# Attention with mixture-of-experts on one core: a constant scale in the exponential, a reordered front, and 25 of 71 expert tiles spread over three steps

## The reference

```python
Q = apply_rope(proj(W_q)); K = apply_rope(proj(W_k)); V = proj(W_v)      # 16 heads of 8
attn = softmax(Q @ K.T / sqrt(8)); attention = (attn @ V) @ W_o.T
w, idx = top_k(xn @ Wg, 2); w = softmax(w)                                # 8 experts, 2 a token
h = relu((layernorm(xn) * gamma[e] + beta[e]) @ W1[e] + b1[e])           # 128 -> 512
expert = h @ W2[e] + b2[e] + xn                                          # 512 -> 128
out = x + attention + sum of w * expert over the two experts
```

## Time and profile before

| | us |
|---|---|
| median of 3 runs | 660.07 |
| lowest, highest run | 659.75, 661.24 |
| the profiled execution's own time | 659.6 |
| span of its profile | 657.7 |
| PE busy, ACT busy, DVE busy in it | 608.5, 548.6, 384.1 |

### The profile page before, as it was taken

The page is one execution under the profiler, slowest core; times in us unless marked ns, Lnnn a source line. Parts: engine busy times, 40 slices in busy tenths (PEclk is TensorE's granted clock), DMA queues, the critical chain, the costliest instruction groups (busy, mean ns, idle before and its releaser), DMA issues.

```text
span 657.7 us, 12339 instructions
## 1 busy us (share of the span) xinstructions
PE 608.5 (93%) x4649; PEld 256.8 (39%) x4649; DVE 384.1 (58%) x1117; ACT 548.6 (83%) x552; POOL 226.1 (34%) x261
## 2 busy tenths in 40 slices
PE   8789889988999999999999999999999999888884
PEld 6223312213545454434454545443444545111112
DVE  4854687888555555587655555558765564335112
ACT  2678899998788888888888888888888888999993
POOL 4399900027753433332433343333234221100000
PEclk9989999999999999999999999999999999999997
DMA  6156411002201202000220120200012111530000
GB/s 229 27 164 179 117 32 33 1 9 53 61 18 29 57 29 57 25 21 17 57 62 17 30 57 29 57 25 21 17 53 54 29 21 45 225 137 32 1 1 34
DMA packets 25425, 35.60 MB, mean 54 GB/s; under 512 B 5472, under 2 KB 15760, under 8 KB 24848
## 3 DMA queue, kind: packets, MB, share of 16 engines
q1 hardware_dynamic: 19936, 23.70, 11.9%
q0 software_dynamic: 4608, 9.45, 5.0%
q10 hardware_dynamic: 816, 1.61, 0.7%
HBM read 17.43 MB, written 8.91 MB: 40 GB/s over the span
## 4 chain that ended last, share of the span: by engine, by line
PE 63%; ACT 22%; DVE 8%; issue 2%; SPq 2%; DMA 1%; DVEq 1%; POOL 0%; ACTq 0%
PE acc L613 23%; ACT ring L825 22%; PE bank L665 11%; PE sc L580 11%; PE bank L657 9%; PE bank L650 2%; PE bank L511 2%; SPq L303 2%; PE bank L674 1%; DVE xn L1169 1%; DVE turned L1148 1%; DVE work L1182 1%; DVE rotated L867 1%; DMA wr<-L_attn_W_k 1%; DVE hl L863 1%
## 5 line engine op out<-in xcount | busy, mean ns | idle before, releaser
L825 ACT ACTIVATE ring<-sc,exp_scale 128x1024 f32<-128x1024 f32 x512 | 534.5, 1130 | 83.2 <-PE sc L580 82.3
L613 PE MATMUL acc<-ring,v 128*9 128x512 f32 x2048 | 268.8, 597 | 2.5 <-issue 2.5
L580 PE MATMUL sc<-qs,ks 32*128 32x512 f16 x1024 | 147.2, 386 | 28.6 <-ACT ring L825 27.4
L456 POOL DMA_INDIRECT token_out<-work,token x72 | 78.4, 1089 | 155.4 <-DVE work L1189 149.1
L446 POOL DMA_INDIRECT work<-normed,token x72 | 70.1, 973 | 159.2 <-DVE work L1175 95.0
L580 PEld LDWEIGHTS sc<-qs,ks 32*128 32x128 f16 x1024 | 40.0, 91 | 145.3 <-ACT ring L825 110.7
L665 PEld LDWEIGHTS bank<-xn,work 128*128 128x128 f32 x576 | 69.7, 191 | 65.1 <-DVE work L1182 37.7
L1182 DVE TENSOR_SCALAR work<-bank,xn 128x128 f32<-128x128 f32 x288 | 80.9, 343 | 22.9 <-PE bank L657 22.8
L665 PE MATMUL bank<-xn,work 128*128 128x128 f32 x576 | 83.2, 287 | 3.1 <-DVE work L1175 3.0
L657 PE MATMUL bank<-work,xn 128*128 128x128 f32 x576 | 77.2, 277 | 2.1 <-DVE norms L888 1.3
L1169 DVE COPY xn<-w_all 128x1158 f32 x72 | 56.5, 785 | 33.2 <-DVE work L1189 32.3
(11 more groups left out here) (175 smaller groups left out, 336.5 us busy)
## 6 DMA issues: line engine op xcount, KB each, us to landing
w_all<-L_ffn_W SPq DMA_DIRECT2D x16, 256.0 KB, 4.9
qs<-hl SPq DMA_DIRECT2D x60, 64.0 KB
ks<-hl SPq DMA_DIRECT2D x60, 64.0 KB
x<-L_attn_x SPq DMA_DIRECT2D x4, 512.0 KB, 7.9
normed<-xn SPq DMA_DIRECT2D x4, 512.0 KB, 3.3
xn<-token_out SPq DMA_DIRECT2D x2, 1024.0 KB, 6.8
w_all<-token_out SPq DMA_DIRECT2D x2, 1024.0 KB, 11.6
out<-x SPq DMA_DIRECT2D x8, 256.0 KB, 2.3
```

The source lines that it names most:

```text
L456: pool.indirect_dma_start(out=y_d[:, :], in_=ys[done % TILE_BUFFERS], in_offset=None, out_offset=bass.IndirectOffsetOnAxis(ap=token[:, 1, ...
L580: last = nc.tensor.matmul(dst, ks[r:r + 32, kb * P:(kb + 1) * P], qs[r:r + 32, at], start=True, stop=not slow)
L613: last = nc.tensor.matmul(acc[qh % 2][32 * j:32 * j + VW, :], v9[:, b, kb, 4 * g + j, :], ring[:, (2 * n + j // 2) % UNITS, j % 2, :], sta ...
L825: nc.scalar.activation(ring[:, (2 * n + u) % UNITS, :, :], sc[u][:, :].rearrange("p (h c) -> p h c", h=2), ACT.Exp, scale=exp_scale[:, 0:1 ...
```

## The change: edits and diff

- The exponential's scale is a number, `SCALE / 2**14`, and not the tile `exp_scale`; ACT no longer waits for it. To allow that, `gains` limits the power for k so that both powers multiply to 2**14 (one more chained DVE instruction and one unchained); `missing_gain` (3 instructions) stands in place of `scales` (4) and tells by `no_room` whether they do; the flag of batch 0 is multiplied by it, and `decide` has one instruction less for later batches. Only the slower branch changes otherwise (it works on widened copies of q and k).
- Front: for piece 0 the plain product comes before the rotated one, on PE and DVE, and its square on ACT with it; the rotated product of piece 3 is made behind `head_norms`; `project_plain` is made before step 0's scores, not in step 0. Six fewer warming matmuls. On POOL, the clearing of `shift` is first, the sorting of `wo` is before the three low parts, and the normalising is x*a+b with an offset made by two more small instructions a batch. Moments of batches 2 and 3 move on DVE to steps 3 and 5, `tops` of batch 0 from step 4 to 8.
- Experts: 71 tiles. 25 of them (tiles 18 to 27, 42 to 51 and 66 to 70, where the step within the batch is from 28 to 61, batch 0 excepted) have three steps: `tile_in(t+1)` and three quarters of `layer_one(t)`; its last quarter and half of `layer_two(t-1)`; the other half. The last expert step is 235 in place of 212. Of the plain steps 101 to 113 and 165 to 177 each now stands between two three-step groups. The flags of batches 2 and 3 are one step later (122, 186).
- End: `LOAD_AT` becomes 237, the merges stand at 241, 244, 247 and 250; the first half of the last batch's projection (step 252) waits on DVE for all merges.

```diff
-GAIN_EXPONENT = 127 + 12 + 63
+SCORE_BITS = 14
+TOP_EXPONENT = 127 + 12 + 63
 ROPE_ORDER = ((0, 0), (0, 1), (1, 0), (1, 1))
-WARM = (10, 18)
-SLOT_TILES = 72
+WARM = (10, 12)
...
-TOP_AT = {4: 0, 11: 1, 15: 2, 19: 3}
+MOMENTS_AT = {3: 2, 5: 3}
+TOP_AT = {8: 0, 11: 1, 15: 2, 19: 3}
...
+FFN_FROM = 54
 FREE_STEPS = [n for n in range(FFN_FROM, STEPS) if n not in PLAIN_AT and n not in PROJECT_AT]
+TWO_STEPS = (((0, FC), None), (None, (0, FC)))
+THREE_STEPS = (((0, 3), None), ((3, FC), (0, 2)), (None, (2, FC)))
 FIRST, SECOND, WEIGHTS_AT = {}, {}, {}
 used = 0
 for t in range(SLOT_TILES):
-    FIRST[FREE_STEPS[used]] = t
-    used += t < SLOT_TILES - DENSE_TILES
-    SECOND[FREE_STEPS[used]] = t - 1
-    WEIGHTS_AT[FREE_STEPS[used]] = t + 2
-    used += 1
-SECOND[FREE_STEPS[used]] = SLOT_TILES - 1
-SECOND = {n: t for n, t in SECOND.items() if t >= 0}
-WEIGHTS_AT = {n: t for n, t in WEIGHTS_AT.items() if t < SLOT_TILES}
+    n = FREE_STEPS[used]
+    wide = n > PER_BATCH and n % PER_BATCH in LONG_IN and FREE_STEPS[used + 1] == n + 1
+    for one, two in THREE_STEPS if wide else TWO_STEPS:
+        if one:
+            FIRST[FREE_STEPS[used]] = (t, *one)
+        if two and t > 0:
+            SECOND[FREE_STEPS[used]] = (t - 1, *two)
+        used += 1
+    if t + 2 < SLOT_TILES:
...
-MERGE_AT = {LOAD_AT + 8 + 5 * b: b for b in range(B)}
+MERGE_AT = {LOAD_AT + 4 + 3 * b: b for b in range(B)}
...
             nc.gpsimd.memset(v9[:, :, :, :, DK:VW].rearrange("p b k h o -> p (b k h) o"), 1.0).then_inc(v_one, 1)
+            nc.gpsimd.memset(shift[:, :], 0.0).then_inc(shift_zero, 1)
             nc.gpsimd.memset(small[:, 10, :], -0.5).then_inc(pool_step, 1)
...
+            def offsets(ts):
+                after(nc.gpsimd.tensor_tensor(small[:, 9, ts], mv[:, ts, 0], small[:, 6, ts], ALU.mult))
+                after(nc.gpsimd.tensor_scalar(small[:, 8, ts], small[:, 9, ts], -1.0, None, ALU.mult))
             def normed(t):
-                nc.gpsimd.tensor_scalar(xn[:, t, :], x[:, t, :], mv[:, t, 0:1], small[:, 6, t:t + 1],
-                                        ALU.subtract, ALU.mult).then_inc(xn_pool, 1)
+                nc.gpsimd.tensor_scalar(xn[:, t, :], x[:, t, :], small[:, 6, t:t + 1], small[:, 8, t:t + 1],
+                                        ALU.mult, ALU.add).then_inc(xn_pool, 1)
             for h in range(2):
                 ts = slice(4 * h, 4 * h + 4)
...
+            nc.gpsimd.tensor_copy(wo_by_head[:, :].rearrange("o (j g d) -> o j g d", j=4, g=4),
+                                  wr[:, 3, :].rearrange("o (g j d) -> o j g d", g=4, j=4)).then_inc(wo_sorted, 1)
             for i, r in enumerate((0, 3, 2)):
                 c, s = ROPE_ORDER[r]
...
-            pool.wait_ge(wo_in, 16)
-            nc.gpsimd.tensor_copy(wo_by_head[:, :].rearrange("o (j g d) -> o j g d", j=4, g=4),
-                                  wr[:, 3, :].rearrange("o (g j d) -> o j g d", g=4, j=4)).then_inc(wo_sorted, 1)
-            nc.gpsimd.memset(shift[:, :], 0.0).then_inc(shift_zero, 1)
...
             pe.wait_ge(bank_taken[1], USE["second half",])
-            for r in range(2):
-                project_front(sc[r][:, CH:2 * CH], r, 1).then_inc(proj, 1)
-                project_front(sc[r][:, 0:CH], r, 0).then_inc(proj, 1)
+            project_front(sc[0][:, 0:CH], 0, 0).then_inc(proj, 1)
+            project_front(sc[0][:, CH:2 * CH], 0, 1).then_inc(proj, 1)
+            project_front(sc[1][:, CH:2 * CH], 1, 1).then_inc(proj, 1)
+            project_front(sc[1][:, 0:CH], 1, 0).then_inc(proj, 1)
...
+            pe.wait_ge(rope_rot, 1)
             project_front(sc[0][:, 0:CH], 2, 0).then_inc(proj, 1)
-            project_front(acc[1][:, :], 3, 1).then_inc(proj, 1)
             values(0, 1)
             pe.wait_ge(head_ok, 1)
             head_norms(0)
+            project_front(acc[1][:, :], 3, 1).then_inc(proj, 1)
             values(0, 2)
             check_bound(0)
             values(0, 3)
...
-                pe.wait_ge(w_ok, t + 1)
-                pe.wait_ge(bank_taken[1], USE["tile", t])
-                enter_bank(0, "one", t)
-                for c in range(FC):
+            def layer_one(t, c0, c1):
+                if c0 == 0:
+                    pe.wait_ge(w_ok, t + 1)
+                    pe.wait_ge(bank_taken[1], USE["tile", t])
+                    enter_bank(0, "one", t)
+                for c in range(c0, c1):
                     last = nc.tensor.matmul(bank[0][:, c * P:(c + 1) * P], w_tile[t % 3][:, c * P:(c + 1) * P],
                                             xsT[t % 2], start=True, stop=True)
...
-            def layer_two(t):
-                pe.wait_ge(bank_taken[0], USE["one", t])
-                enter_bank(1, "two", t)
-                for c in range(FC):
+                if c1 == FC:
+                    last.then_inc(bank_full[0], 1)
...
                         project_rotated()
                     if n == 0:
...
-                                         ACT.Exp, scale=exp_scale[:, 0:1]).then_inc(e_ok, 1)
+                                         ACT.Exp, scale=SCALE / (1 << SCORE_BITS)).then_inc(e_ok, 1)
...
-                nc.vector.tensor_scalar(gain[:, :].bitcast(I32), half_exp[:, :], -float(1 << 23),
-                                        float(GAIN_EXPONENT << 23), ALU.mult, ALU.add).then_inc(gain_ok, 1)
...
-            def scales():
-                link(nc.vector.tensor_scalar(ungain[:, :].bitcast(I32), half_exp[:, :], float(1 << 23),
-                                             float((254 - GAIN_EXPONENT) << 23), ALU.mult, ALU.add))
-                link(nc.vector.tensor_tensor(bound_scale[:, 0:1], ungain[:, 0:1], ungain[:, 1:2], ALU.mult))
-                nc.vector.tensor_scalar(exp_scale[:, 0:1], bound_scale[:, 0:1], SCALE, 1e30, ALU.mult, ALU.min
-                                        ).then_inc(scale_ok, 1)
-                nc.vector.tensor_tensor(bound_scale[:, 1:2], bound_scale[:, 0:1], bound_scale[:, 0:1], ALU.mult
-                                        ).then_inc(scale_ok, 1)
+                nc.vector.tensor_scalar(room[:, :], half_exp[:, 0:1], float(127 + SCORE_BITS - 12 - 63), None,
+                                        ALU.add)
+                link(nc.vector.tensor_scalar(gain_exp[:, :], half_exp[:, :], -1.0, float(TOP_EXPONENT), ALU.mult,
+                                             ALU.add))
+                link(nc.vector.tensor_tensor(gain_exp[:, 1:2], gain_exp[:, 1:2], room[:, :], ALU.min))
+                nc.vector.tensor_scalar(gain[:, :].bitcast(I32), gain_exp[:, :], float(1 << 23), None, ALU.mult
+                                        ).then_inc(gain_ok, 1)
+            def missing_gain():
+                link(nc.vector.tensor_tensor(no_room[:, :], room[:, :], gain_exp[:, 1:2], ALU.subtract))
+                nc.vector.tensor_scalar(missing[:, :].bitcast(I32), no_room[:, :], 127.0, float(1 << 23), ALU.add,
+                                        ALU.mult)
...
-                    link(nc.vector.tensor_scalar(flag_f[:, 0:1], flag_f[:, B:B + 1], (SAFE / SCALE) ** 2, None,
-                                                 ALU.is_le))
+                    link(nc.vector.scalar_tensor_tensor(out=flag_f[:, 0:1], in0=flag_f[:, B:B + 1],
+                                                        scalar=(SAFE / SCALE) ** 2, in1=no_room[0:1, :],
+                                                        op0=ALU.is_le, op1=ALU.mult))
...
-                v.wait_ge(proj, rotated_made)
-                times(rotated[:, :], rotated_of, r, sin)
+                if rotated_made < plain_made:
+                    v.wait_ge(proj, rotated_made)
+                    times(rotated[:, :], rotated_of, r, sin)
                 v.wait_ge(proj, plain_made)
                 v.wait_ge(sq_ok, i + 1)
                 times(turned[r % 2][:, :], plain_of, r, cos).then_inc(rope_out, 1)
+                if rotated_made > plain_made:
+                    v.wait_ge(proj, rotated_made)
+                    times(rotated[:, :], rotated_of, r, sin).then_inc(rope_rot, 1)
+                    v.wait_ge(rope_rot, 1 if i == 0 else 2)
                 add_up(i, r)
...
             link(split_high(1))
             nc.vector.tensor_tensor(hl[:, 1, 1, 0:CH], turned[1][:, :], hl[:, 1, 0, 0:CH], ALU.subtract
                                     ).then_inc(low_dve, 1)
...
+            missing_gain()
             bound(0)
             decide(0)
...
+                nc.vector.tensor_scalar(wide[0][:, :], qs[:, :], missing[:, :], None, ALU.mult).then_inc(m_wide[b], 1)
+                nc.vector.tensor_copy(wide[1][:, :], ks[:, :]).then_inc(m_wide[b], 1)
                 for n in range(4 * TB):
                     v.wait_ge(m_mm[b], 4 * TB * base + n + 1)
...
+                if b == B - 1:
+                    v.wait_ge(merged, B)
...
+                if n in MOMENTS_AT:
+                    moments_of(MOMENTS_AT[n])
...
-                    if FIRST[n] + 1 < SLOT_TILES:
```

(32 more changed lines are left out.)

71 lines of the change are left out of this document (44 added, 27 removed).

## The result

The changed kernel takes 632.79 us (median, 631.96 to 634.26, 4 runs) against 659.91 (658.87 to 661.24) for the kernel before beside it: ratio 0.959, 95% interval 0.9563 to 0.9618. The forecast was 632. The profiled execution is the slowest of the four: 634.26, span 632.4.

What follows compares the result with a forecast made beforehand. A loop over PE and ACT, counting asides and exponential duration half, bounds most expert steps; ACT alone bounds the last. From 659.6: -21.1 experts, -0.1 and -1.9 front, -4.2 steps 8 to 53, giving 632 us; range 623 to 645.

Steps and rivals of the forecast that it cites:

- The loop: PE and ACT in the expert steps: two steps take 3.91 plus an aside; the number as scale takes off 0.15.
- I take the value by the square, the nearest row: Exponential on ACT: saving read from a square without scale tile, 0.09 in duration and 0.065 in interval; 0.15 taken.
- the first rival: Rival (1): the operand's whole price, 0.09, falls in the interval too; 5.0 less, 627 us; chance 0.15.
- Steps 54 to 235: Loop 342.2, asides at half weight 89.2, pairs 1.6, norms and bound 3.1, splits 1.5: 437.6 us.
- rival (3): DVE stays late at splits, masks and in the front: 3.9 and 2 more, 638 us; chance 0.10.
- Pair, group, bare step: Expert steps: a pair at 4.91, a three-step group at 6.86, bare steps at 1.88 us.
- The splits' waits: Layer two behind eight splits: 5.4 us of waiting for DVE, 0.7 each; spreading removes them, 1.5 kept.
- The front: First steps: -0.1 for `gains`, -1.9 for `project_plain` made before the first scores; steps 8 to 53: -4.2 us.
- The end: Steps 236 to 254 take 36.8 us; up to 3 steps of merge delay are hidden, cost 0.
- (2): Rival: the constant scale brings nothing, the loop stays 3.91; 652 to 653 us; chance 0.08.
- (4): Rival: granted clock falls in the three-step groups, 5.5 more each, with all 25 some 765 us; chance 0.02.
- (5): Rival: the fast branch is not taken, were `no_room` 0; far slower; chance 0.01.

Runs made afterwards that it cites:

- b_number_cut: The kernel before with the number as exponential scale, and DVE's four instructions per split of batches 1 to 3 on 8 of 512 columns: 632.92 us.
- experiments 1, 4 and 5: The runs b_number (640.77 us), a_pairs (636.91 us) and b_number_cut (632.92 us), in this order.
- experiment 1: The run b_number: the kernel before with only the exponential's scale tile replaced by a number, 640.77 us.
- a_pairs: The changed kernel with no three-step groups, all 71 tiles in pairs, experts ending at step 210: 636.91 us, ratio 0.9641.
- b_number: The kernel before with a number in place of the tile as the exponential's scale, nothing else changed: 640.77 us, ratio 0.9707.
- experiment 9: The changed kernel with weight rows turned in step 19, not 5, and the second warming batch at 18 matmuls, not 12: 632.3 us, ratio 0.9552.
- experiments 1 to 3: Number as scale in the kernel before, 640.77 us; scale tile back in the changed kernel, 653.89; zero bias tile added in the kernel before, 686.19.

## Why the prediction was right

**The number** is within 1 us, and the mechanism is the one foretold. That it is so close is partly luck: in steps 54 to 235 the loop gave 3.6 us more than foretold and other stretches took 4.3 more. Its terms, one by one:

- *The loop.* Right in kind, too small in size: 0.15 was taken, 0.18 to 0.19 measured (3.91 to 3.72), with 0.09 in the duration and 0.09 in the interval. The step that failed is "I take the value by the square, the nearest row". The square's 0.10 of fixed part came from one neighbour distance behind a shorter instruction; the first rival ("one fetch should cost one time") had the price right. Over steps 54 to 235 it is worth 0.04 x 182 / 2 = 3.6 us.
- *Steps 54 to 235*: 437.6 foretold, 438.3 measured, though the loop is faster than assumed. The prediction's own formula with a loop of 3.72 shows where it was given back. Steps 63 to 91 should take 71.1 (29 x 1.86, 14 tiles and two output projections) and take 71.0. Steps 101 to 125 should take 25 x 1.86 + 7 x 1.22 + 4 x 0.53 = 57.2, with 1.0 for the norms 58.2; they take 59.3, and so do 165 to 189. Steps 57 to 62 take 17.2 here and 16.2 in b_number_cut. So these three stretches are some 3 longer than the formula and b_number_cut have them, and the 1.5 that the sum kept for the splits is not in the trace. In steps 57 to 62 it is DVE's lateness, with these two rows (in b_number_cut 0.41 at the norms and none over 0.2 at layer two):

```profile
155.28 1.13 PE L699 MATMUL bank<-xn,work 128*128 128x128 f32 x8 [0.70 <-DVE work L1223]
...
158.88 1.13 PE L689 MATMUL bank<-work,xn 128*128 128x128 f32 x8 [0.58 <-DVE norms L922]
```

  In the split stretches it isn't: PE waits there for DVE once in each, 0.40 at the norms, which the 58.2 has. And b_number_cut, with DVE's split work left out, is over the same formula by more: 46.5 + (10 x 1.15 + 11 x 1.08) / 2 + 2.1 + 1.0 = 61.3, and 62.7 measured. What makes the 1.1 a stretch stays open. The formula leaves out two things there: that of the asides of alternate steps the loop follows the larger (1.06 and 0.86 against 0.93 and 0.64), and the squares that ACT makes between exponentials:

```profile
269.20 1.94 ACT L857 ACTIVATE ring<-sc 128x1024 f32<-128x1024 f32 x2 [0.23 <-PE sc L610]
271.02 0.63 ACT L863 ACTIVATE wr<-turned 128x512 bf16<-128x512 f32 x1
```

  So the loop's error of 3.6 was cancelled by these, and by smaller amounts elsewhere: rival (1) had the price, and rival (3) was right for 1.0 of it.
- *Pair, group, bare step*: 4.91, 6.86 and 1.88 foretold; 4.87, 6.82 and 1.86 measured. So a wide group costs 6.82 - 4.87 - 1.86 = 0.09 more than a pair and a bare step, the 0.07 of the prediction.
- *The splits' waits.* That wide groups remove them is shown (experiments 1, 4 and 5). Their size was put at 5.4, 0.7 for each of eight splits, and the wide groups are worth 4.1 net. But the 5.4 was a remainder: in before's trace the wait of 0.70 at layer two stands behind four of the eight (steps 105, 113, 169, 177), 2.8 in all. What the prediction missed is that these waits would have grown with the faster exponential (4.1 to 6.3, experiment 1): a term read from the old trace was carried into a kernel whose pace differs. "In the new order `columns` stands ahead of the split" holds only with the wide groups; in a_pairs it doesn't, and the wait is there.
- *The front.* -1.9 and -0.1 foretold for steps 0 to 7. Step 8 starts at 44.09 here and at 45.99 in b_number, which has the same scale and the same kind of start: -1.9. But its parts were wrong. Between these two kernels PE's wait for the weight rows ends 2.5 earlier (40.36 for 42.84; with early starts 38.88 in a_pairs for 40.91 in b_number_cut, 2.0). Of that, 1.1 stands before the first exponential (24.98 for 26.12; 0.9 with early starts) and is the fewer warming matmuls' (experiment 9), which the prediction had as idle time and a risk. The reordering is left with some 1.2, where 1.9 were foretold. Steps 8 to 53: -4.2 foretold, 104.1 - 99.7 = 4.4 measured.
- *The end.* Cost 0 foretold for the merges, and 0 it is. The last merge and `add_out` on DVE (for the earlier trace rows):

```profile
608.70 4.37 DVE L1247 SCALAR_TENSOR_TENSOR x<-w_all,small,x 128x128 f32<-128x128 f32 x16
...
617.03 0.69 DVE L1210 TENSOR_TENSOR x<-bank,x 128x512 f32<-128x512 f32 x1 [3.95 <-PE bank L709]
```

  The merges are done at 613.07, and DVE waits 3.95 for PE, not PE for DVE. Steps 236 to 254: 36.8 foretold, 37.1 measured, against 36.4 in b_number. The difference stands in step 236 alone (2.64 for 1.84), behind the last tile's layer two.
- *The other rivals.* (2), the scale brings nothing, is refuted by experiments 1 to 3. (4), the clock: the granted clock is 1.00 through the groups (the first window above). (Its price was also added up wrong: 25 x 5.5 is 137.5, which gives some 770 and not 765.) (5): the time itself shows that the fast branch was taken.

The rest of the change is small: by the medians, the number as scale is worth 19.1, the front and the tile less 3.9 (a_pairs against b_number), the wide groups 4.1.

**Still open**: why the higher clock is granted at 4 to 6 us in one execution and at 10 in the next; what makes the 1.1 us in each split stretch.

## What to carry to other kernels

When two engines hand work back and forth, neither's busy share gives the price of a change: write down the loop, see whose duration stands in it whole and whose half, and then look for the stretches where a third engine sets the pace, because a gain in the loop stops there, and the waits read from the old trace grow. A full PE is no proof of a PE bound: 98% busy (402.14 of 409.59 us) still had 5.06 - 4.85 = 0.21 us a pair to give, and the changed kernel, at 4.87, has used it up. Before an operation is moved, see which instructions run side by side only because they stand together.
